# Joint reciprocal, weighting and floor for four heads in the attention stage of a vision transformer block

## The reference

```python
h = tok_ref(x, W, b)                                    # patches to 192 channels
q, k, v = heads(Wq), heads(Wk), heads(Wv)               # of layernorm(h), 12 heads of 16
q, k = apply_rope(q, cos, sin), apply_rope(k, cos, sin)
scores = einsum('bhsd,bhtd->bhst', q, k) / sqrt(hd)
weights = erf(scores) + 1.0
weights = where(mask, weights, 0.0)                     # lower triangle
y = einsum('bhst,bhtd->bhsd', weights, v) / maximum(weights.sum(-1), EPS)
h = h + y.reshape(B, S, D) @ Wproj.T
h = h + ffn_ref(layernorm(h), ...)                      # 8 experts, top 2, and a shared one
```

## Time and profile before

| what | value |
|---|---|
| median of 3 runs | 3384.44 us (3378.82 to 3385.17) |
| profiled execution | 3376.83 us, of it the span of the trace 3374.7 us |
| mean granted TensorE clock over the span | 0.945 |
| TensorE matmul busy, share of the span | 3091.8 us, 92% |
| VectorE busy | 2446.8 us, 73% |
| ScalarE busy | 1526.7 us, 45% |
| GpSimd busy | 1377.0 us, 41% |

### The profile page before, as it was taken

How to read it: one execution, slowest core, us unless ns; L and a number is a source line. 1 busy time by engine, 2 the same in 40 slices (tenths; PEclk the granted TensorE clock), 3 DMA queues, 4 the chain that set the end, 5 groups by cost and what they waited for, 6 DMA issues and landing times. The chain is left out here.

```text
span 3374.7 us, 70939 instructions
## 1 busy us (share of the span) xinstructions
PE 3091.8 (92%) x25828; PEld 2110.6 (63%) x25828; DVE 2446.8 (73%) x4893; ACT 1526.7 (45%) x3223; POOL 1377.0 (41%) x1172
## 2 busy tenths in 40 slices
PE   6999999999999999998059999899999999999997
PEld 5777777777777777766025555556666556566664
DVE  6999999999999999997766555554555455455543
ACT  2444444444444444443024444444555455455443
POOL 1332233223332332322202555536666555655664
PEclk9899999999999999986579999999999999999999
DMA  3333333323332333322122222245554555545442
GB/s 104 77 75 78 73 87 80 81 66 87 89 76 68 81 89 75 75 46 54 45 67 67 74 67 78 59 95 101 77 96 71 98 71 97 101 69 97 77 75 42
DMA packets 460505, 260.36 MB, mean 77 GB/s; under 512 B 337967, under 2 KB 441759, under 8 KB 456063
## 3 DMA queue, kind: packets, MB, share of 16 engines
q1 hardware_dynamic: 392448, 196.41, 24.3%
q0 software_dynamic: 54464, 49.01, 10.3%
q10 hardware_dynamic: 13262, 10.66, 0.9%
HBM read 107.98 MB, written 68.15 MB: 52 GB/s over the span
## 5 line engine op out<-in xcount | busy, mean ns | idle before, releaser
L1309 DVE SCALAR_TENSOR_TENSOR ffn_hidden<-ffn_up,ffn_silu 128x490 f32<-128x490 f32 (+2 forms) x534 | 350.6, 670 | 676.2 <-ACT ffn_silu L1290 510.9
L690 POOL TENSOR_TENSOR weights<-weights,x_pair 128x400 f32<-128x400 f32 x384 | 396.3, 1032 | 828.7 <-DVE weights L556 810.1
L1290 ACT ACTIVATE ffn_silu<-ffn_gate 128x490 f32<-128x490 f32 (+2 forms) x534 | 301.9, 582 | 735.6 <-PE ffn_up L1253 541.6
L1487 POOL DMA_INDIRECT out_rows<-done,ids x256 | 407.4, 1591 | 407.6 <-ACT done L1593 346.4
L608 DVE RECIPROCAL recip<-x_product 128x200 f32<-128x200 f32 x384 | 534.2, 1391 | 0.0
L1274 PE MATMUL ffn_out<-ffn_w_hi,ffn_hidden_hi 128*128 128x192 f16 (+1 forms) x2124 | 525.6, 247 | 3.9 <-DVE ffn_hidden_lo L1302 2.0
L1275 PE MATMUL ffn_out<-ffn_w_lo,ffn_hidden_hi 128*128 128x192 f16 (+1 forms) x2124 | 522.8, 246 | 0.0
L1276 PE MATMUL ffn_out<-ffn_w_hi,ffn_hidden_lo 128*128 128x192 f16 (+1 forms) x2124 | 522.7, 246 | 0.0
L748 PE MATMUL bank<-w_tok,patches 128*128 128x192 f32 x1536 | 327.2, 370 | 56.8 <-ACT normed_t L411 32.7
L1302 DVE TENSOR_TENSOR ffn_hidden_lo<-ffn_hidden,ffn_hidden_hi 128x490 f16<-128x490 f32 (+2 forms) x534 | 356.3, 667 | 15.9
L1284 ACT CAST ffn_hidden_hi<-ffn_hidden 128x490 f16<-128x490 f32 (+2 forms) x534 | 320.7, 601 | 91.9 <-DVE ffn_hidden L1309 90.7
(11 more groups left out here) (176 smaller groups left out, 6862.2 us busy)
## 6 DMA issues: line engine op xcount, KB each, us to landing
patches<-in_patches SPq DMA_DIRECT2D x32, 1176.0 KB, 5.2
ffn_raw<-in_w SPq DMA_DIRECT2D x18, 768.0 KB
dram_x_t<-x_t SPq DMA_DIRECT2D x32, 392.0 KB, 3.7
x_t<-dram_x_t SPq DMA_DIRECT2D x24, 512.0 KB
base<-dram_h SPq DMA_DIRECT2D x24, 384.0 KB, 4.2
out_rows<-sums ACTq DMA_DIRECT2D x24, 384.0 KB, 4.6
v_held<-v SPq DMA_DIRECT2D x64, 102.0 KB, 2.3
dram_h<-h SPq DMA_DIRECT2D x32, 192.0 KB
```

What stands on the lines that cost most here:

```text
L690: nc.gpsimd.tensor_tensor(weights[:, n % 4], weights[:, n % 4], x_pair[:, n % 4, ::-1], ALU.mult)\
L1290: nc.scalar.activation(T.silu[:, m % 2, 0:n], T.gate[m % 2][:, 0:n], ACT.Silu, scale=1.0 / (TOKEN_SCALE * WEIGHT_SCALE)).then_inc(T.silued, 1)
L1309: nc.vector.scalar_tensor_tensor(T.hidden[:, m % 2, 0:n], T.up[m % 2][:, 0:n], HIDDEN_SCALE / (TOKEN_SCALE * WEIGHT_SCALE), T.silu[:, m % ...
L1487: nc.gpsimd.indirect_dma_start(out=dram["out"][:, :], out_offset=bass.IndirectOffsetOnAxis(ap=ids[i][0:height, t, 0:1], axis=0), in_=done[ ...
```

## The change

Two pairs (four heads of one image) become a quad, of which a unit has six (`QUADS`).

- **One reciprocal for a quad.** VectorE multiplies the x of both pairs in one instruction (`multiply_pairs`), multiplies the two products (`multiply_all`), takes one reciprocal (`invert`), and multiplies it crosswise with the two products (`share`), which gives each pair its own reciprocal. `weigh` and `floor` then do both pairs in one instruction of twice the width. The copies to `x_pair` are scaled by 2^14 more, and `GUARD` is changed, to keep the fourfold product in range.
- **VectorE's order.** Even slots have `multiply_all(q)`, `weigh(q - 1)`, `invert(q)`; odd slots have `floor(q - 1)`, `share(q)`, `multiply_pairs(q + 1)`. The slot's other work stands behind these. `outputs` of the second image moves from slot 1 to slot 4, the residual add from 5 to 6, the second norm from 6 to 7.
- **Six buffers** for `x_pair` and `weights` in place of four, and scores two pairs ahead in place of one on TensorE and ScalarE.
- **Rotation** of two tiles in one instruction for each step, in place of one tile.
- **TensorE and ScalarE**: the transposes of y move from slot 4 to 5, the projection from 5 to 6, the transposes of x2 from 9 to 10, and ScalarE copies `normed_t` ahead of the Gelu of slot 3.
- **GpSimd** waits for `weighted` only ahead of the first pair of a quad.

```diff
-    (1, 2), (4, 5, 6, 7), (8, 11), (9, 10), (12, 13), (16, 17), (19,), (0, 3, 14, 15))
+    (1, 2), (4, 5, 6, 7), (8, 9), (10, 11), (12, 13), (16, 17), (19,), (0, 3, 14, 15))
+QUADS = PAIRS // 2
...
-                        act.wait_ge(weighted, pair - 3)
-                    nc.scalar.activation(x_pair[:, n % 4], score[n % 2][:, :, 0:PACKED], ACT.Copy,
-                                         scale=QK_SCALE ** -2).then_inc(copied_out, 1)
+                        act.wait_ge(weighted, QUADS * u + n // 2 - 2)
+                    nc.scalar.activation(x_pair[:, n % 6], score[n % 2][:, :, 0:PACKED], ACT.Copy,
+                                         scale=PAIR_SCALE * QK_SCALE ** -2).then_inc(copied_out, 1)
...
+            def multiply_pairs(u, q, opens):
+
+                dve.wait_ge(copied_out, PAIRS * u + 2 * q + 2)
+                if not opens:
+                    dve.wait_ge(shared, QUADS * u + q - 1)
+                x = x_pair[:, 2 * q % 6:2 * q % 6 + 2]
+                nc.vector.scalar_tensor_tensor(x_product[:, q % 2], x[:, :, 0], SCORE_SCALE / 2 / PAIR_SCALE, x[:, :, 1],
+                                               ALU.mult, ALU.mult).then_inc(multiplied_x, 1)
+
+            def multiply_all(u, q):
+
+                dve.wait_ge(multiplied_x, QUADS * u + q + 1)
+                nc.vector.tensor_tensor(x_all[:, q % 2], x_product[:, q % 2, 0], x_product[:, q % 2, 1], ALU.mult)\
+                  .then_inc(multiplied_all, 1)
+
+            def invert(u, q):
+
+                dve.wait_ge(multiplied_all, QUADS * u + q + 1)
+                nc.vector.reciprocal(recip[:, q % 2], x_all[:, q % 2]).then_inc(inverted, 1)
+
+            def share(u, q, opens):
+
+                dve.wait_ge(inverted, QUADS * u + q + 1)
+                if not opens:
+                    dve.wait_ge(weighted, QUADS * u + q - 1)
+                nc.vector.tensor_tensor(recip_pair[:, q % 2], x_product[:, q % 2, ::-1], over(recip[:, q % 2], [128, 2, PACKED]),
+                                        ALU.mult).then_inc(shared, 1)
+
+            def weigh(u, q):
+
+                dve.wait_ge(crossed, PAIRS * u + 2 * q + 2)
+                dve.wait_ge(shared, QUADS * u + q + 1)
+                w = weights[:, 2 * q % 6:2 * q % 6 + 2]
+                nc.vector.tensor_tensor(w, w, recip_pair[:, q % 2].unsqueeze(2).to_broadcast([128, 2, 2, PACKED]),
...
+            def floor(u, q):
...
+                dve.wait_ge(weighted, QUADS * u + q + 1)
+                masked = weights[:, 2 * q % 6:2 * q % 6 + 2].rearrange("p n c x -> p (n c) x")[:, :, 0:MASKED]
+                nc.vector.scalar_tensor_tensor(masked, masked, FLOOR, over(causal[:], [128, 4, MASKED]),
...
+                    q = n // 2
+                    if n % 2 == 0:
+                        if pairs:
+                            multiply_all(u, q)
+                        if pairs and q >= 1:
+                            weigh(u, q - 1)
+                        if n == 0 and has_prev:
+                            weigh(u - 1, QUADS - 1)
+                        if pairs:
+                            invert(u, q)
+                    else:
+                        if pairs and q >= 1:
+                            floor(u, q - 1)
+                        if n == 1 and has_prev:
+                            floor(u - 1, QUADS - 1)
+                        if pairs:
+                            share(u, q, kind == "first" and q < 2)
+                        if pairs and q < QUADS - 1:
+                            multiply_pairs(u, q + 1, kind == "first" and q + 1 < 2)
...
-                    if n == 1 and has_prev:
-                        outputs(u - 1, 1)
...
+                        for i in range(2):
+                            dve.wait_ge(free[QK[t + i] % NB], fills(kind, u, QK[t + i]))
...
+                    if n == 4 and has_prev:
+                        outputs(u - 1, 1)
...
-                if not opens:
+                if n % 2 == 0 and not opens:
 
                     pool.sem_inc(spacer, 1)
-                    pool.wait_ge(weighted, PAIRS * u + n)
+                    pool.wait_ge(weighted, QUADS * u + n // 2)
...
-                pe.wait_ge(floored, PAIRS * u + n + 1)
+                pe.wait_ge(floored, QUADS * u + n // 2 + 1)
```

More of the change, by code:

```diff
@@ L276, in attention @@
         qk_raw = sb("qk_raw", [128, 4, 2 * D])
-        by_cos = [sb(f"by_cos{s}", [128, 2 * NH, 2, HD // 2]) for s in range(2)]
-        by_sin = [sb(f"by_sin{s}", [128, 2 * NH, 2, HD // 2]) for s in range(2)]
+        by_cos = sb("by_cos", [128, 2, 2 * NH, 2, HD // 2])
+        by_sin = sb("by_sin", [128, 2, 2 * NH, 2, HD // 2])
         rotated = sb("rotated", [128, 4, 2 * NH, HD])
@@ L431, in turn @@
                         act.wait_ge(copied_out, pair + 1)
-                        if kind != "first" or n >= 4:
-                            act.wait_ge(attended, pair - 3)
-                        nc.scalar.activation(weights[:, n % 4], x_pair[:, n % 4], ACT.Gelu, scale=SCORE_SCALE)\
+                        if kind != "first" or n >= 6:
+                            act.wait_ge(attended, pair - 5)
+                        nc.scalar.activation(weights[:, n % 6], x_pair[:, n % 6], ACT.Gelu, scale=SCORE_SCALE / PAIR_SCALE)\
                           .then_inc(gelued, 1)
-                    if n == 3 and has_next:
-                        for k, pos in enumerate(LN1T):
-                            copy_out(pos, normed_t[:, k * UT:(k + 1) * UT], KD)
                     if n in (2, 3, 7, 8) and has_tokens:
@@ L588, in turn @@
                 for n in range(PAIRS):
-                    if pairs:
-                        pair = PAIRS * u + n
-                        if n < PAIRS - 1:
-                            if kind != "first" or n >= 1:
-                                dve.wait_ge(inverted, pair)
-                            multiply_x(u, n + 1)
-                        elif has_next:
-                            dve.wait_ge(inverted, pair)
-                            multiply_x(u + 1, 0)
-                        if n >= 1:
-                            weigh(u, n - 1)
@@ L601, in turn @@
-                    if n == 0 and has_prev:
-                        weigh(u - 1, PAIRS - 1)
-                    if pairs:
-                        dve.wait_ge(multiplied_x, pair + 1)
-                        if kind != "first" or n >= 2:
-                            dve.wait_ge(weighted, pair - 1)
-                        nc.vector.reciprocal(recip[:, n % 2], x_product[:, n % 2]).then_inc(inverted, 1)
-                        if n >= 1:
-                            floor(u, n - 1)
-                    if n == 0 and has_prev:
-                        floor(u - 1, PAIRS - 1)
+                    q = n // 2
@@ new lines, in turn @@
+                    if n % 2 == 0:
[16 more added lines that the diff above has]
+                            multiply_pairs(u, q + 1, kind == "first" and q + 1 < 2)
+                        if n == PAIRS - 1 and has_next:
+                            multiply_pairs(u + 1, 0, kind == "pro")
@@ new lines, in turn @@
+                            dve.wait_ge(free[QK[t + i] % NB], fills(kind, u, QK[t + i]))
+                        settle()
+                        src = qk_raw[:, t:t + 2, :].rearrange("p i (g f) -> p i g f", f=HD // 2)
+                        for c, out in enumerate((by_cos, by_sin)):
+                            table = tables[:, :, c, :].unsqueeze(2).to_broadcast([128, 2, 4 * NH, HD // 2])
+                            step(nc.vector.tensor_tensor(out[:].rearrange("p i h c f -> p i (h c) f"), src, table, ALU.mult))
@@ L752, in turn @@
                 for n in range(PAIRS):
-                    if pairs and n < PAIRS - 1:
-                        if n + 1 == PAIRS // 2:
+                    if pairs and n < PAIRS - 2:
+                        if n + 2 == PAIRS // 2:
                             pe.wait_ge(qk_turned[1][slot], 32 * turned_uses(kind, u, prior, slot, False))
-                        scores(kind, u, n + 1, qk_t[slot])
-                    if n == PAIRS - 1 and has_next:
-                        pe.wait_ge(qk_turned[0][prev], 32 * turned_uses(kind, u, prior, slot, True))
-                        scores("first" if kind == "pro" else "mid", u + 1, 0, qk_t[prev])
+                        scores(kind, u, n + 2, qk_t[slot])
+                    if n >= PAIRS - 2 and has_next:
+                        if n == PAIRS - 2:
+                            pe.wait_ge(qk_turned[0][prev], 32 * turned_uses(kind, u, prior, slot, True))
+                        scores("first" if kind == "pro" else "mid", u + 1, n + 2 - PAIRS, qk_t[prev])
                     if pairs and n >= LAG:
```

80 lines of the change are left out of this document (32 added, 48 removed).

## The result

The changed kernel takes 3758.32 us (median of 4 runs, 3749.07 to 3772.58) against 3381.63 before (4 runs): 1.1119 times as long, interval [1.1079, 1.1159]. The forecast, 3542, had the direction and 160 of the 377 us; its range ended at 3640. The profiled execution took 3761.22 us with a span of 3759.4.

A forecast was written before the change was run, and what follows sets the result against it. VectorE and TensorE are both nearly full, so a loop between them binds: 37.6 + 13.0 + 2.8 collisions = 53.4 us a unit, 5.6 over 47.8, times 29 units 162 us; predicted 3542 us, range 3400 to 3640.

The forecast's parts named there:

- The loop: Quad 5's floor through TensorE and ScalarE to slot 3's rotation, then VectorE to the next such floor: 50.6 us a unit.
- the wait that was to close it: TensorE idle for several us before the attend of pair 10 in slot 2, released by quad 5's floor.
- The collisions: GpSimd's second cross of a quad delays VectorE behind reciprocals of slots 0, 4, 6, 8: 4 x 0.7 = 2.8 us.
- The one forecast for slot 7: Second cross of slot 6's quad, put into slot 7 by the small root between the crosses: 0.7 us.
- VectorE's own work: VectorE's instructions in a unit: 4.7 us less by its sum alone, falling to about 43 us.
- The clock: Lower clock, 1.2 GHz, on TensorE's tile after the floor wait: 1.5 us of the 13.0 kept; without it the loop is 49.1.
- at nothing: Costed at zero: six buffers, scores two ahead, y transposes behind `outputs` in slot 5, q and k's transposing DMAs.
- More of the same: Rival: collisions of 0.82 or more, or lower clock over more of the 13 us: 3600 to 3675 us; chance 0.08.
- TensorE becomes the bound, faster: Rival: the loop does not bind, TensorE sets 46.1 us a unit, 49 us less, 3328 us; chance 0.11.

The follow-up runs named there:

- x3: Changed kernel with five unused matmuls ahead of each of TensorE's waits at slot 5's y transposes and slot 10's attend of pair 6: 3619.27 us.
- x10: Changed kernel with pairs 10 and 11 attended behind slot 3's first q and k products, LAG 5, and slot 4's outputs ahead of the rotation: 3401.71 us.
- x15: x10 with the second patch tile ahead of normed's transposes, pairs 10 and 11 attended after these, two fill matmuls in each of slots 1 and 10: 3369.05 us.
- x9: Changed kernel with pairs 10 and 11 attended behind slot 3's first q and k products, every other attend one slot later (LAG 5): 3657.94 us.
- x14: x9 with four unused fill matmuls added in slot 10 alone, ahead of the attend there: 3428.26 us.
- x13: x9 with four unused fill matmuls added in slot 5 alone, ahead of the y transposes: 3412.73 us.

## Why the prediction was right in direction and wrong in size

- **The loop** was right in its lengths: VectorE stands 9.0 us a unit before and for the rotation (6.6 + 2.4; some 8 forecast), and floor to rotation took 14.2 on the mean (13.0). But the wait that was to close it, several us of TensorE ahead of pair 10, is 0.5 us in the changed kernel, since TensorE is late by the lower clock; it is there, 4.95 us, once the clock is held (x3). Taken out with the clock held up, the loop is worth 4.1 us a unit. The direction was no luck: x3 has most of the clock back and is still 7% slower, although TensorE still has 5.6 us a unit of waits, so that the work added there does not set the time.
- **The collisions** were right in sum, 3.04 us a unit for 2.8, and struck the norm, the rotation and a floor as forecast. The one forecast for slot 7 fell into a wait of VectorE; in its place the one of slot 10 struck, though not `outputs` but `share` in slot 11 (1.40 us where it takes 0.56). The four in the rows lose 0.71 to 0.84 us, where I took 0.7 for each. By the Trainium skill, "SBUF — State Buffer", section "Who interferes with whom", such a pair blocks each other for the whole instruction; by it I had estimated 3.3 us. The rows agree: the floor at 705.30 takes 1.43 instead of 0.70.
- **VectorE's own work** was nearly right: 60.25 less 14.7 of waits and 3.0 of collisions is 42.5 us, forecast some 43. That forecast took all of the 47.8 before for work, of which 1.3 were waits; so 4.0 us were saved of 4.7.
- **The clock** is the step that failed. I kept its cost at the 1.5 us within the 13.0 us from floor to rotation, put the y transposes "at nothing", because TensorE "has the slack of its wait at pair 10", and did not count the wait of pair 6 for its quad's floor. These two waits are 2.0 and 1.8 us, and in the changed kernel the clock falls within 2 us of the end of each, in every unit from 5 to 25. The lower clock takes 29.5 us a unit instead of 3.4. TensorE's work, some 43.5 us at the higher clock (x10's 46.3 less half of its 5.5 at the lower), becomes 55.8 us; slot 6 takes 7.5 us instead of 4.5, and VectorE waits for the projection and the high parts inside the stretch from rotation to floor, which I had counted without waits (40.4 forecast, 44.9 above, 46.2 on the mean).
- **The terms together.** Forecast 53.4 us a unit, measured 60.25. Of the 6.9 missing, x3 returns 4.9 by holding the clock for most of the unit, with 3.2 us of work added. The other 1.9 are x3's 41.5 us from rotation to floor (40.4 forecast) and its 13.8 from floor to rotation (13.2 to 14.7; 13.0 forecast). The last step of the sum does not come out: 3539 and 7.6 are 3547, not 3542, 5 us of the 216 that are missing.
- **The rivals.** "More of the same" had the lower clock over another 1.5 to 3 us of the 13, a tenth of the 26 us that came, and in the wrong place. "TensorE becomes the bound, faster" is refuted for the kernel as changed; x15 comes nearest to it: TensorE is busy 292 of 300 us, and the kernel is 0.4% faster than the one before, where the rival's 49 us would be 1.5%.

## What to carry to other kernels

Where two engines are nearly full, a saving on one becomes waiting time on the other, and on TensorE a wait can cost many times its length (here the edit that removed one of 1.16 us gave 9.2 us a unit, x9 to x10): price each new wait ahead of small matmuls with the stretch at the lower clock behind it. When work is made in larger batches, the first consumer of a batch loses slack; give it that back in the order (here one slot of lag, the attends of pairs 10 and 11 and one function moved, 357 us) before the batch is judged. A clock problem is shown by adding useless matmuls in a wait: if more work takes less time and the granted clock rises with it, it was the clock.

## What was unexpected of the hardware

- The edit that took away one wait of 1.16 us took 28.3 us at the lower clock down to 5.5 (x9, x10), and yet the same wait had none behind it in 12 of 21 units of x14. The Trainium skill, "TensorE: Matmul & The Clock Gate", section "HAM oscillation — how this bites in real kernels", tells of a wait in each tile (there of 3 to 5 us, for a DMA) that lets the clock fall each time. With the 1.16 us here x9 agrees, x14 does not.
- The clock fell, and stayed at 0.57 on the mean over 19.7 us, while TensorE was busy throughout (x13, slots 10 to 2 of unit 12). Being busy with small matmuls did not hold the clock there; the same slots of x14 ran at 1.00 (unit 11).
- A cross shortened to 4 columns of each head left 0.3 us or less of VectorE's 3.0 us of collisions a unit.
